# A mixture-of-factored-experts upper layer on TensorE: straight code that reads its operands in place, instead of loops that read staging buffers

## The chip, the cores and the metric

The kernel runs on one core of one Trainium2 chip. The metric is the device time of one launch in microseconds (us). The reference names used below are TensorE (PE, with PEld for its weight loads), VectorE (DVE), ScalarE (ACT), GpSimd (POOL) and SyncE (SP, which starts the DMA transfers). All data are float32.

## The reference

Three residual blocks follow each other: cross attention to a context, causal self attention, and a feed-forward part that is a mixture of experts with top-2 routing. Only the last is touched. Each of its two layers does this for every token:

```python
def kmoe(x_flat, W_router, A, B, scale, bias, d_in1, d_in2, d_out1, d_out2, top_k):
    logits = x_flat @ W_router.T
    vals, idx = jax.lax.top_k(logits, top_k)
    probs = jax.nn.softmax(vals, axis=-1)
    xs = x_flat.reshape(-1, d_in1, d_in2)
    Ag = A[idx]
    Bg = B[idx]
    Y = jnp.einsum('nkoi,nij,nkpj->nkop', Ag, xs, Bg)
    out = jnp.einsum('nkop,nk->nop', Y, probs).reshape(-1, d_out1 * d_out2)
    return out * scale + bias
...
h = kmoe(x_flat, W_up, A_up, B_up, scale_up, bias_up, D1, D2, F1, F2, TOP_K)
h = jax.nn.gelu(h, approximate=False)
y = kmoe(h, W_down, A_down, B_down, scale_down, bias_down, F1, F2, D1, D2, TOP_K)
```

There are 64 experts, D1 = D2 = 32 and F1 = F2 = 64. A pair of rows of 512 makes one item of 32x32, so there are 1024 items, of which the kernel takes 256 at a time: four blocks, T = 0 to 3.

## The kernel before

After the two attention stages (lines below 1230) comes `mixture`. Its **upper layer** runs over the four blocks T; its **lower layer** does so after it. For each block T of the upper layer TensorE does, in this order:

- **gather**: 16 units (`gather_up`, L2122), each of 32 small matmuls that multiply one-hot choices with the table of the factors A (v = 0) or B (v = 1), so that each item's factors appear in PSUM. ACT (L2006) and DVE (L1843) copy each unit out into the factor tiles `up[0]` and `up[1]`. A unit waits for the copies of the unit two before it.
- transposes of the next block's rows (`rows`, L1453), the router products of the lower layer for the block before (`logits_dn`, L2100) and of the upper layer for the next block (`logits_up`, L1460), and `fold_dn` (L2108);
- **steps**: 16 steps, two at a time. `first_up` (L2139) makes 64 small matmuls for two steps, ACT copies each result to `mid` (`mid_out`, L2022), `second_up` (L2157) makes 16 small matmuls for each step, DVE adds the bias (L1852), ACT applies gelu (L2033, L2027);
- transposes of the next choices (`transpose_choices`, L1468).

What is written once in the PE program and run in loops: the whole body for T (`pe.Fori(0, T_N)`), within it the gather (one lap is four units, four laps) and the steps (one lap is two steps, eight laps). Parts that some T does without stand in `pe.If`. Since a loop's body names fixed addresses, the operands that change from lap to lap come from **staging buffers** at fixed addresses: POOL copies four rows of the table into `tab_st` (`stage_table`, L1767), two rows of the factors into `st_a` and `st_b` for each step (`stage_a` L1775, `stage_b` L1784), and ACT copies the input's rows into `st_hh` (`stage_x`, L2014). PE waits for these copies on `s_ts`, `s_sta`, `s_stb` and `s_stx`. The cross attention before it is written out without loops on PE, self attention is one loop and one written-out last lap, and the lower layer is a loop again.

All orders are written by hand; each engine runs its own list, and semaphores tie them together.

Of the kernel before, what the change touches and what calls it, by code (L numbers as in the profile page):

```python
# [1243 lines left out]
def mixture_parts(sem, arena, over, area, low, top_area, early, ps, ident, h_at, tables):  # L1244
# [60 lines left out]
    s_xfe, s_gelu, s_stx = sem("mo_xfe"), sem("mo_gelu"), sem("mo_stx")  # L1305
# [11 lines left out]
    s_ts, s_ex, s_oc = sem("mo_ts"), sem("mo_ex"), sem("mo_oc")  # L1317
    s_sta, s_stb = sem("mo_sta"), sem("mo_stb")
# [229 lines left out]
    f.s_stx = s_stx  # L1548
# [18 lines left out]
    f.s_ts = s_ts  # L1567
    f.s_ex = s_ex
    f.s_oc = s_oc
    f.s_sta, f.s_sad, f.AHEAD = s_sta, s_sad, AHEAD  # L1570
# [29 lines left out]
def mixture(nc, block, arena, early, ps, a, first, rest, out):  # L1600
# [58 lines left out]
    s_stx = first.s_stx  # L1659
# [15 lines left out]
    s_ts = first.s_ts  # L1675
    s_ex = first.s_ex
    s_oc = first.s_oc
    s_sta, s_sad, AHEAD = first.s_sta, first.s_sad, first.AHEAD
# [27 lines left out]
    def _(sp):  # L1706
# [28 lines left out]
        sp.wait_ge(s_stx, STEPS * T_N + AHEAD)  # L1735
# [18 lines left out]
    def _(pool):  # L1754
# [8 lines left out]
        def stage_table(T, q):  # L1763
            for v in range(2):
                if T or q:
                    pool.wait_ge(s_gu, 16 * T + 2 * (q - 1) + v + 1)
                pool.tensor_copy(tab_st[v], tab_up[v][:, 4 * q:4 * q + 4, :]).then_inc(s_ts, 1)  # L1767

        def stage_a(T, n):
            if n == 0:  # L1770
                for e in range(2):
                    pool.wait_ge(s_geu[e], 16 * T + 15 + CREDIT)
            if T or n >= 2:
                pool.wait_ge(s_s1, STEPS * T + n - 1)
            pool.tensor_copy(four(st_a[n % 2]), up[0][:, :, rows_of(n), :].rearrange("p m r o -> p m (r o)"))\  # L1775
                .then_inc(s_sta, 1)

        def stage_b(T, n):
            if n == 0:
                for e in range(2):  # L1780
                    pool.wait_ge(s_geu[e], 16 * T + 16 + CREDIT)
            if T or n >= 2:
                pool.wait_ge(s_s2, STEPS * T + n - 1)
            pool.tensor_copy(four(st_b[n % 2]), up[1][:, :, rows_of(n), :].rearrange("p m r o -> p m (r o)"))\  # L1784
                .then_inc(s_stb, 1)

# [14 lines left out]
        pool.sem_inc(s_sta, AHEAD)  # L1801
        pool.sem_inc(s_stb, AHEAD)
        pool.memset(euler, EULER).then_inc(s_fold, 1)
        stage_table(0, 0)
        pool.wait_ge(s_fold, 2)
        exponential("up", 0)
        for T in range(T_N):
            for q in range(1, 8):
                stage_table(T, q)
            stage_a(T, 0)  # L1810
            stage_a(T, 1)
            for n in range(STEPS):
                stage_b(T, n)
                if n + 2 < STEPS:
                    stage_a(T, n + 2)
                if n == 6 and T + 1 < T_N:
                    exponential("up", T + 1)
                if n == 10 and T:
                    exponential("dn", T - 1)
                if n == 8 and T == 0:  # L1820
                    rest.rstd(pool)
            if T + 1 < T_N:
                stage_table(T + 1, 0)
# [9 lines left out]
    def _(vec):  # L1833
# [23 lines left out]
        def gather_out_dn(T, v, g):  # L1857
            if g == 1:
                if T and v == 0:
                    vec.wait_ge(s_sad, UP + STEPS * T + AHEAD - 2)  # L1860
                else:
                    vec.wait_ge((s_sta, s_stb)[v], UP + STEPS * T + AHEAD)
# [137 lines left out]
    def _(act):  # L2000
        def gather_out(T, q, v):
            if T and q == 0:
                act.wait_ge((s_sta, s_stb)[v], STEPS * T + AHEAD)
# [3 lines left out]

        def stage_x(T, n):

            if n == 0:  # L2010
                act.wait_ge(s_xt, 2 * T + 2)
            if T or n >= 2:
                act.wait_ge(s_s1, STEPS * T + n)
            act.copy(st_hh.rearrange("p (u z) -> p u z", u=2)[:, :, 0:P].rearrange("p u (t x) -> p u t x", t=2),  # L2014
                     xt[:, :, 2 * n:2 * n + 4, :].rearrange("p t (u r) j -> p u t (r j)", u=2)).then_inc(s_stx, 2)
# [19 lines left out]
        def gather_out_dn(T, v, g):  # L2035
            if g == 0:
                if T and v == 0:
                    act.wait_ge(s_sad, UP + STEPS * T + AHEAD - 2)
                else:
                    act.wait_ge((s_sta, s_stb)[v], UP + STEPS * T + AHEAD)  # L2040
# [12 lines left out]
        act.sem_inc(s_stx, AHEAD)  # L2053
        act.sem_inc(s_sad, UP + AHEAD - 2)
        act.sem_inc(s_ohe["dn"][0], CREDIT)
        for T in range(T_N):
# [3 lines left out]
            stage_x(T, 0)  # L2060
# [33 lines left out]
    def _(pe):  # L2094
# [16 lines left out]
        def gather_up(v, g):  # L2111

            pe.wait_ge(s_ts, g * 2 + v + 1)
            for e in range(2):
                pe.wait_ge(s_geu[e], g * 2 + v - 1 + CREDIT)
            apart(pe, SPARE)
            for o in range(4):
                for c in range(C):
                    for hf in range(2):
# [3 lines left out]
                                         tab_st[v][r, o, :], x, start=True, stop=True)  # L2123
            last.then_inc(s_gu, 1)

        def first_up(n):


            pe.wait_ge(s_sta, n + 2 + AHEAD)
            pe.wait_ge(s_stx, n + 2 + AHEAD)  # L2130
            apart(pe, SPARE)
            for u in range(2):
                xs = st_h[u][:, 0:P].rearrange("p (m j) -> p m j", m=4)
                for m in range(4):
                    for c in range(C):
# [203 lines left out]
```

## Time and profile before

| | us |
|---|---|
| median of 3 runs | 1332.3 (1331.91 to 1333.19) |
| the profiled execution, whole | 1332.9 |
| its span on the core | 1330.9 |
| PE busy within the span | 1239.7 |
| DVE, ACT, POOL busy | 809.8, 439.1, 227.8 |
| first to last instruction of the upper layer on PE | 868.7 to 1115.7 |

The rows are in the section after the change. Times of rows count from the span's start. On PE a matmul of float32 appears in the trace as two MATMUL records and two LDWEIGHTS records (the 2048 matmuls of L2122 are 4096 records of each kind), a transpose as one of each. "Idle before <-issue" means that the engine stood still and no semaphore, DMA or other engine that the profile shows had just released it. Queue q8 in the DMA part carries packets of kind "instruction".

### The profile page before, as it was taken

To read this page: it belongs to the slowest core of one execution; us is meant where nothing else is said; L and a number is where in the kernel's file an instruction comes from. 1 tells how busy PE (TensorE), PEld (TensorE's weight loads), DVE (VectorE), ACT (ScalarE), POOL (GpSimd) and SP (SyncE) were. 2 spreads that over 40 slices of the span, in tenths; PEclk is the share of its full clock that TensorE was granted. 3 is DMA by queue.
4 is the path that set the end of the run, shared out by engine and by line. 5 is a ranking of instruction groups with operands and counts; after the bars stand their busy time and mean duration, and the time that the engine had idled before them with its cause. 6 is when DMAs were issued, how large, how long until landed. Compare 5 with 4: busy or idle time off the path is not lost.

```text
span 1330.9 us, 61276 instructions
## 1 busy us (share of the span) xinstructions
PE 1239.7 (93%) x27820; PEld 808.8 (61%) x27820; DVE 809.8 (61%) x1523; ACT 439.1 (33%) x863; POOL 227.8 (17%) x373
## 2 busy tenths in 40 slices
PE   9999999999999999999999997978889888889886
PEld 6764333333333334677666774757778777779775
DVE  5567767767777771555565564546574846464766
ACT  2223211321132112222122221235463646354564
POOL 1000000000000001222122221116151532212212
PEclk9899999999999999999999999998999999895998
DMA  7976899899989973411101112201221306334012
GB/s 295 319 225 190 310 297 311 277 316 288 311 276 316 293 273 90 80 64 63 48 16 63 63 47 70 57 33 80 111 114 43 127 4 249 139 149 190 26 37 95
DMA packets 68176, 211.50 MB, mean 159 GB/s; under 512 B 14544, under 2 KB 30928, under 8 KB 53616
## 3 DMA queue, kind: packets, MB, share of 16 engines
q1 hardware_dynamic: 68080, 210.16, 46.9%
q8 instruction: 68, 1.11, 0.4%
q14 instruction: 28, 0.23, 0.1%
HBM read 172.37 MB, written 37.75 MB: 158 GB/s over the span
## 4 chain that ended last, share of the span: by engine, by line
PE 77%; DVE 10%; issue 5%; DMA 3%; POOL 2%; ACT 2%; SPq 1%; DVEq 0%; POOLq 0%; ACTq 0%
PE ps L715 14%; PE ps L564 10%; PE ps L1088 8%; PE ps L2171 6%; PE ps L235 4%; PE ps L2122 4%; PE ps L1202 4%; PE ps L1109 4%; DVE arena L576 4%; PE ps L479 3%; PE ps L2100 2%; PE ps L2213 2%; PE ps L705 2%; PE ps L2197 2%; DVE arena L1852 2%
## 5 line engine op out<-in xcount | busy, mean ns | idle before, releaser
L576 DVE STREAM_TRANSPOSE arena<-arena 128x448 f32<-128x448 f32 (+1 forms) x512 | 263.6, 577 | 101.8 <-PE ps L564 83.6
L564 PE MATMUL ps<-arena 32*64 32x400 f32 (+1 forms) x4096 | 202.7, 506 | 1.4 <-DVE arena L576 0.7
L715 PE MATMUL ps<-arena 128*64 128x512 f32 x832 | 189.2, 598 | 0.0
L564 PEld LDWEIGHTS ps<-arena 32*64 32x64 f32 x4096 | 75.3, 130 | 97.8 <-issue 51.7
L715 PEld LDWEIGHTS ps<-arena 128*64 128x64 f32 x832 | 55.6, 136 | 121.3 <-issue 111.9
L599 ACT ACTIVATE arena<-ps,arena 128x384 f32<-128x384 f32 x64 | 36.3, 582 | 276.5 <-DVE arena L590 276.5
L1088 PE MATMUL ps<-arena 128*128 128x256 f32 x512 | 114.7, 382 | 0.8 <-ACT arena L1023 0.8
L1088 PEld LDWEIGHTS ps<-arena 128*128 128x128 f32 x512 | 96.9, 191 | 17.4 <-issue 3.3
L2022 ACT COPY arena<-ps 128x512 f32<-128x512 f32 x128 | 75.1, 588 | 84.8 <-PE ps L2171 58.7
L1852 DVE SCALAR_TENSOR_TENSOR arena<-ps,arena 128x512 f32<-128x512 f32 x64 | 69.8, 1116 | 43.8 <-PE ps L2157 43.5
L2171 PE MATMUL ps<-arena 64*64 64x32 f32 x4096 | 84.2, 236 | 5.8 <-issue 5.7
L888 POOL TENSOR_TENSOR arena<-arena 128x1024 f32<-128x1024 f32 x8 | 18.9, 2367 | 406.5 <-PE ps L715 406.5
L2171 PEld LDWEIGHTS ps<-arena 64*64 64x64 f32 x4096 | 78.0, 153 | 10.2 <-issue 7.3
L2122 PE MATMUL ps<-arena 64*32 64x128 f32 x4096 | 69.1, 273 | 13.0 <-issue 6.7
L2122 PEld LDWEIGHTS ps<-arena 64*32 64x32 f32 x4096 | 58.1, 105 | 24.4 <-issue 19.6
L956 DVE SCALAR_TENSOR_TENSOR arena<-ps,arena 128x512 f32<-128x512 f32 x32 | 20.6, 686 | 81.0 <-PE ps L1099 81.0
L1791 POOL COPY arena<-arena 128x512 f32<-128x512 f32 x64 | 41.9, 659 | 162.1 <-ACT arena L2043 89.7
L2197 PE MATMUL ps<-arena 64*64 64x256 f32 x1024 | 62.1, 395 | 6.0 <-DVE arena L1865 3.5
L479 PE MATMUL ps<-arena 128*128 128x256 f32 x256 | 60.5, 391 | 0.0
L1843 DVE COPY arena<-ps 128x512 f32<-128x512 f32 x64 | 43.7, 692 | 27.1 <-PE ps L2122 26.9
L235 PE MATMUL ps<-arena 128*128 128x512 f32 x128 | 60.2, 605 | 0.0
L906 POOL TENSOR_TENSOR arena<-arena 128x512 f32<-128x512 f32 x32 | 33.4, 1044 | 149.3 <-DVE arena L973 149.3
(153 smaller groups left out, 1842.6 us busy)
## 6 DMA issues: line engine op xcount, KB each, us to landing
arena<-ctx SPq DMA_DIRECT2D x64, 1024.0 KB
arena<-ctx SPq DMA_DIRECT2D x32, 768.0 KB
arena<-q_n SPq DMA_DIRECT2D x64, 256.0 KB, 11.3
h_n<-arena SPq DMA_DIRECT2D x16, 1024.0 KB, 4.4
arena<-h_n SPq DMA_DIRECT2D x16, 1024.0 KB, 10.0
arena<-x SPq DMA_DIRECT2D x16, 512.0 KB, 4.5
arena<-ctx SPq DMA_DIRECT2D x32, 256.0 KB
x_n<-arena SPq DMA_DIRECT2D x16, 512.0 KB, 3.5
```

The costliest lines, as they stand in the source:

```text
L235: x = pe.matmul(ps[:, par, :], early.ats[:, c, par::2], early.xwv[:, c, :], start=c == 0, stop=c == DC - 1)
L479: last = pe.matmul(ps[:, QB + h, m % 2 * QROWS:(m % 2 + 1) * QROWS], wqk[:, c, m * P:(m + 1) * P], lnt[n][:, c, :], start=c == 0, stop=c = ...
L564: last = pe.matmul(ps[b * SEQ:(b + 1) * SEQ, tb, 0:WIDTH[tb]], qs[p % 2][r, db, b * SEQ:(b + 1) * SEQ], z[r, at % RING, b, 0:WIDTH[tb]], s ...
L576: vec.transpose(z[:, at % RING, :, g * 224:g * 224 + nt * 32].rearrange("p b (j t) -> p b j t", t=32), slots[slot_of(k)][:, :, 0:nt, db * ...
L715: last = pe.matmul(ps[b * SEQ:(b + 1) * SEQ, OB, :], probt[:, j, b * SEQ:(b + 1) * SEQ], slot[:, b, jj, :], start=j == 0, stop=j == TILES - 1)
L1088: last = pe.matmul(ps[:, bank, m % 2 * QROWS:(m % 2 + 1) * QROWS], w[n][:, c, m * P:(m + 1) * P], lnt[:, c, :], start=c == 0, stop=c == DC ...
L1109: last = pe.matmul(ps[e * SEQ:(e + 1) * SEQ, 2 + pair, s2 * 256:(s2 + 1) * 256], lnt[:, c, at:at + SEQ], w["swv"][:, c, :].rearrange("p (m ...
L1852: vec.scalar_tensor_tensor(h[:, q, :, at].rearrange("p j g -> p g j"), ps[:, b:b + 2, :].rearrange("p b (g x) -> p (b g) x", x=2 * F1)[:, ...
L2022: act.copy(mid[u].rearrange("p (b x) -> p b x", b=2), ps[:, 2 * u:2 * u + 2, 0:256]).then_inc(s_me, 1)
L2122: last = pe.matmul(ps[c * R:(c + 1) * R, 4 * v + hf, o * P:(o + 1) * P], tab_st[v][r, o, :], x, start=True, stop=True)
L2171: last = pe.matmul(ps[k * F1:(k + 1) * F1, 2 * u + t, g * D1:(g + 1) * D1], st_h[u][rows_t, g * F1:(g + 1) * F1], two(st_a[u])[rows_t, k, ...
L2197: last = pe.matmul(ps[t * E:(t + 1) * E, 2 * (g % 4) + hf, o % 2 * 2 * P:(o % 2 + 1) * 2 * P], tab_dn[v][r, o, :], x, start=True, stop=True)
```

## The change

On PE the loops over T, over the gather's units and over the steps, and the `If`s, are replaced by Python loops, so that every matmul of the upper layer stands in the program by itself, with its own addresses. `gather_up` then reads the tables `tab_up` directly, `first_up` reads `xt` and `up[0]`, and `second_up` reads `up[1]`. The copies `stage_table`, `stage_a`, `stage_b` (POOL) and `stage_x` (ACT) go, and with them the semaphores `s_ts`, `s_sta`, `s_stx`; those who waited on them to know that a buffer is free wait for `s_s1` and `s_s2`, the ends of the first and second products. The number and shape of the matmuls stays. The lower layer keeps its loops and its staging.

```diff
         def transposed(vec, T, t):
-            vec.wait_ge(s_stx, STEPS * T + AHEAD)
+            vec.wait_ge(s_s1, STEPS * T)
...
-            for q in range(1, 8):
-                stage_table(T, q)
-            stage_a(T, 0)
-            stage_a(T, 1)
-            for n in range(STEPS):
-                stage_b(T, n)
-                if n + 2 < STEPS:
-                    stage_a(T, n + 2)
...
-                vec.wait_ge((s_sta, s_stb)[v], STEPS * T + AHEAD)
+                vec.wait_ge((s_s1, s_s2)[v], STEPS * T)
...
-            stage_x(T, 0)
-                if n + 2 < STEPS:
-                    stage_x(T, n + 2)
...
-        def gather_up(v, g):
-            pe.wait_ge(s_ts, g * 2 + v + 1)
+        def gather_up(T, v, q):
             for e in range(2):
-                pe.wait_ge(s_geu[e], g * 2 + v - 1 + CREDIT)
-            apart(pe, SPARE)
+                pe.wait_ge(s_geu[e], 16 * T + 2 * q + v - 1 + CREDIT)
...
-                                         tab_st[v][r, o, :], x, start=True, stop=True)
+                                         tab_up[v][r, 4 * q + o, :], x, start=True, stop=True)
...
-        def first_up(n):
-            pe.wait_ge(s_sta, n + 2 + AHEAD)
-            pe.wait_ge(s_stx, n + 2 + AHEAD)
+        def first_up(T, n):
+            u = n % 2
+            if n == 0:
+                pe.wait_ge(s_xt, 2 * T + 2)
...
-        def second_up(n, u):
-            pe.wait_ge(s_stb, n + 1 + AHEAD)
...
-                                             four(st_b[u])[rows_d, 2 * t + c, r * F1:(r + 1) * F1], start=True, stop=True)
+                                             up[1][rows_d, 2 * t + c, 2 * n + r, :], start=True, stop=True)
...
         def steps_up(T):
-            with pe.Fori(T * 8, T * 8 + 8) as i:
-                first_up(i * 2)
-                second_up(i * 2, 0)
-                second_up(i * 2 + 1, 1)
+            for n in range(0, STEPS, 2):
+                first_up(T, n)
+                first_up(T, n + 1)
+                second_up(T, n)
+                second_up(T, n + 1)
...
-        with pe.Fori(0, T_N) as T:
+        for T in range(T_N):
...
-            with pe.Fori(T * 4, T * 4 + 4) as j:
-                for r in range(2):
-                    gather_up(0, j * 2 + r)
-                    gather_up(1, j * 2 + r)
+            for q in range(8):
+                for v in range(2):
+                    gather_up(T, v, q)
...
-            with pe.If(T < T_N - 1):
+            if T + 1 < T_N:
```

What stands in PE's program for the gather and the steps before, written once for all four blocks (`ps` is PSUM, `arena` is SBUF; L2122 is the gather, L2139 and L2157 the two products):

```order
L2248 ISA
L2115 REGISTER_ALU
L2122 MATMUL ps<-arena 32x128 x32
L2113 REGISTER_ALU
...
L2248 COMPARE_AND_BRANCH
...
L2219 ISA
L2139 MATMUL ps<-arena 32x64 x64
L2146 REGISTER_ALU
L2157 MATMUL ps<-arena 64x64 x32
L2219 ISA
L2219 COMPARE_AND_BRANCH
```

The same place in the changed kernel, for block T = 1 (L2071 is the gather, L2051 `logits_dn`, L2086 and L2101 the two products):

```order
L2071 MATMUL ps<-arena 32x128 x512
L1453 MATMUL ps<-arena 128x128 x16
L2051 MATMUL ps<-arena 64x128 x128
L1460 MATMUL ps<-arena 128x64 x16
L2059 MATMUL ps<-arena 128x64 x2
L2086 MATMUL ps<-arena 32x64 x64
L2101 MATMUL ps<-arena 64x64 x32
L2086 MATMUL ps<-arena 32x64 x64
L2101 MATMUL ps<-arena 64x64 x32
```

Branches and register instructions are gone from this part; the gather stands there as 512 matmuls in a row where 4 times 32 stood, and the pair of products eight times where it stood once, and all of it once more for each T.

POOL's program in one block T before (L1767 copies the table, L1775 and L1784 the factors, L1761 is the exponential of a routing):

```order
L1767 COPY arena<-arena 128x128 x16
L1775 COPY arena<-arena 128x512 x2
L1784 COPY arena<-arena 128x512
L1775 COPY arena<-arena 128x512
L1784 COPY arena<-arena 128x512
```

and all that POOL has left to do in the changed kernel's upper layer:

```order
L1774 MEMSET arena 128x2
L1757 TENSOR_TENSOR arena<-arena 128x2 x2
L150 TENSOR_SCALAR arena<-arena 128x2
L152 TENSOR_TENSOR arena<-arena 128x2
L1757 TENSOR_TENSOR arena<-arena 128x2 x5
```

The exponentials and the last attention lap's small statistics stay; every copy between them is gone.

## Rows read from the trace of the kernel before

**Rows 1.** The page: busy time (share of the span) xinstructions by engine

```profile
PE 1239.7 (93%) x27820; PEld 808.8 (61%) x27820; DVE 809.8 (61%) x1523; ACT 439.1 (33%) x863; POOL 227.8 (17%) x373
```

**Rows 2.** Busy time in stretches: attention, then the upper layer's T = 0 to 3

```profile
core 0: us, PE busy (x) PEld busy (x) DVE busy (x) ACT busy (x) POOL busy (x), PEclk, DMA share, GB/s
24.00:560.00 536.00, 528.51 (x5962) 244.66 (x5961) 344.94 (x740) 126.96 (x353) 16.27 (x24) 0.99 0.83 265
868.60:935.30 66.70, 50.59 (x2617) 44.83 (x2616) 36.52 (x57) 33.93 (x56) 26.35 (x51) 0.92 0.16 64
935.30:996.30 61.00, 55.16 (x2884) 49.11 (x2884) 37.99 (x63) 33.17 (x57) 24.24 (x50) 1.00 0.26 104
996.30:1058.00 61.70, 55.09 (x2884) 49.11 (x2884) 38.90 (x65) 33.77 (x58) 24.25 (x50) 1.00 0.22 85
1058.00:1114.00 56.00, 47.89 (x2822) 42.43 (x2822) 34.53 (x49) 30.34 (x51) 23.12 (x47) 1.00 0.19 75
1196.00:1230.00 34.00, 33.71 (x1365) 31.90 (x1369) 17.10 (x29) 14.74 (x27) 10.12 (x16) 0.52 0.46 179
```

**Rows 3.** PE in order of time, T = 1: start, us, line, records [idle before]

```profile
935.36 4.49 PE L2122 MATMUL ps<-arena 64*32 64x128 f32 x256 [1.53 <-DVE arena L1438]
...
950.37 4.25 PE L2122 MATMUL ps<-arena 64*32 64x128 f32 x256 [0.28 <-issue]
...
968.17 1.48 PE L2139 MATMUL ps<-arena 32*32 32x64 f32 x128
969.80 1.32 PE L2157 MATMUL ps<-arena 64*64 64x64 f32 x64
...
992.78 0.69 PE L2157 MATMUL ps<-arena 64*64 64x64 f32 x32 [0.26 <-DVE arena L1852]
```

**Rows 4.** PE in order of time, T = 0, the loop's first lap

```profile
868.65 2.76 PE L2122 MATMUL ps<-arena 64*32 64x128 f32 x153
874.14 1.89 PE L2122 MATMUL ps<-arena 64*32 64x128 f32 x103 [2.72 <-issue]
...
897.39 6.88 PE L1460 MATMUL ps<-arena 128*128 128x64 f32 x32 [5.38 <-issue]
```

**Rows 5.** The same view at the upper layer's end and in the lower layer

```profile
1115.69 14.86 PE L2197 MATMUL ps<-arena 64*64 64x256 f32 x240 [0.77 <-ACT arena L1440]
...
1144.26 0.43 PE L2213 MATMUL ps<-arena 128*32 128x32 f32 x12 [1.74 <-issue]
```

**Rows 6.** DMA queues in the stretch 24 to 560: packets, MB, share

```profile
q8 instruction: 47, 0.77, 0.6%
```

**Rows 7.** DMA queues in the stretch 936 to 1113 (all that there are)

```profile
q1 hardware_dynamic: 2569, 15.60, 22.1%
q14 instruction: 6, 0.05, 0.1%
```

**Rows 8.** DMA from 891.6 to 895.0, to 895.3, to 898.5, to 898.8

```profile
q8 instruction: 1, 0.02, 2.1%
...
q8 instruction: 2, 0.03, 3.8%
...
q8 instruction: 2, 0.03, 2.0%
...
q8 instruction: 3, 0.05, 3.0%
```

**Rows 9.** PE in order of time, logits of T = 1 at full clock

```profile
956.81 7.27 PE L2100 MATMUL ps<-arena 64*64 64x128 f32 x256
964.01 3.79 PE L1460 MATMUL ps<-arena 128*128 128x64 f32 x32
```

**Rows 10.** Groups by line: busy us, mean ns | idle before it, releasers

```profile
L2122 PE MATMUL ps<-arena 64*32 64x128 f32 x4096 | 69.1, 273 | 13.0 <-issue 6.7 <-DVE arena L1843 4.3 <-DVE arena L1438 1.5
```

**Rows 11.** One copy that goes, and further down who waited for it

```profile
L1784 POOL COPY arena<-arena x64: 604/618/625, 890.7 to 1109.3; 128x512 f32<-128x512 f32 x64
...
  PE ps L2157: 5.2, 7
```

More of the change, by code:

```diff
@@ L1674, in mixture @@
     s_ohe = first.s_ohe
-    s_ts = first.s_ts
     s_ex = first.s_ex
     s_oc = first.s_oc
-    s_sta, s_sad, AHEAD = first.s_sta, first.s_sad, first.AHEAD
+    s_sad, AHEAD = first.s_sad, first.AHEAD
     s_stb = first.s_stb
@@ L1734, in _ @@
                 sp.wait_ge(s_out, QUADS * 32)
-        sp.wait_ge(s_stx, STEPS * T_N + AHEAD)
+        sp.wait_ge(s_s1, STEPS * T_N)
         for q in range(4):
@@ L1761, in exponential @@
             pool.tensor_tensor(ex[k], euler, diff[k], ALU.pow).then_inc(s_ex, 1)
[L1763 to L1785, printed above, removed]
         def stage_b_dn(T, n):
@@ L1807, in _ @@
         for T in range(T_N):
-            for q in range(1, 8):
-                stage_table(T, q)
-            stage_a(T, 0)
-            stage_a(T, 1)
-            for n in range(STEPS):
-                stage_b(T, n)
-                if n + 2 < STEPS:
-                    stage_a(T, n + 2)
[L1816 to L1821, printed above, removed]
-            if T + 1 < T_N:
-                stage_table(T + 1, 0)
+            if T + 1 < T_N:
+                exponential("up", T + 1)
+            if T == 0:
+                rest.rstd(pool)
+            if T:
+                exponential("dn", T - 1)
         for T in range(T_N):
@@ L1858, in gather_out_dn @@
             if g == 1:
-                if T and v == 0:
+                if T == 0:
+                    vec.wait_ge((s_s1, s_s2)[v], UP)
+                elif v == 0:
                     vec.wait_ge(s_sad, UP + STEPS * T + AHEAD - 2)
                 else:
-                    vec.wait_ge((s_sta, s_stb)[v], UP + STEPS * T + AHEAD)
+                    vec.wait_ge(s_stb, UP + STEPS * T + AHEAD)
             vec.wait_ge(s_gd[v], 8 * T + g + 1)
@@ L2002, in gather_out @@
             if T and q == 0:
-                act.wait_ge((s_sta, s_stb)[v], STEPS * T + AHEAD)
+                act.wait_ge((s_s1, s_s2)[v], STEPS * T)
             act.wait_ge(s_gu, 16 * T + 2 * q + v + 1)
@@ L2036, in gather_out_dn @@
             if g == 0:
-                if T and v == 0:
+                if T == 0:
+                    act.wait_ge((s_s1, s_s2)[v], UP)
+                elif v == 0:
                     act.wait_ge(s_sad, UP + STEPS * T + AHEAD - 2)
                 else:
-                    act.wait_ge((s_sta, s_stb)[v], UP + STEPS * T + AHEAD)
+                    act.wait_ge(s_stb, UP + STEPS * T + AHEAD)
             act.wait_ge(s_gd[v], 8 * T + g + 1)
@@ L2122, in gather_up, with second_up @@
                         last = pe.matmul(ps[c * R:(c + 1) * R, 4 * v + hf, o * P:(o + 1) * P],
-                                         tab_st[v][r, o, :], x, start=True, stop=True)
+                                         tab_up[v][r, 4 * q + o, :], x, start=True, stop=True)
             last.then_inc(s_gu, 1)
-        def first_up(n):
-            pe.wait_ge(s_sta, n + 2 + AHEAD)
-            pe.wait_ge(s_stx, n + 2 + AHEAD)
[L2131 to L2135, printed above, removed]
-                        rows_c = slice(c * R, (c + 1) * R)
-                        for k in range(2):
-                            q = 2 * (c % 2) + k
-                            last = pe.matmul(ps[q * R:(q + 1) * R, 2 * u + c // 2, m * F1:(m + 1) * F1],
-                                             xs[rows_c, m, :],
-                                             four(st_a[u])[rows_c, m // 2 * 2 + k, m % 2 * F1:(m % 2 + 1) * F1],
-                                             start=True, stop=True)
-                last.then_inc(s_s1, 1)
-        def second_up(n, u):
-            pe.wait_ge(s_me, n + 1 + AHEAD)
-            pe.wait_ge(s_stb, n + 1 + AHEAD)
-            pe.wait_ge(s_bias, n + 1 + AHEAD)
-            apart(pe, SPARE)
+        def first_up(T, n):
+            u = n % 2
+            if n == 0:
+                pe.wait_ge(s_xt, 2 * T + 2)
+            for m in range(4):
+                t, row = m // 2, 2 * n + m % 2
+                for c in range(C):
+                    rows_c = slice(c * R, (c + 1) * R)
+                    for k in range(2):
+                        q = 2 * (c % 2) + k
+                        last = pe.matmul(ps[q * R:(q + 1) * R, 2 * u + c // 2, m * F1:(m + 1) * F1],
+                                         xt[rows_c, t, row, :], up[0][rows_c, 2 * t + k, row, :], start=True, stop=True)
+            last.then_inc(s_s1, 1)
+        def second_up(T, n):
+            u = n % 2
+            pe.wait_ge(s_me, STEPS * T + n + 1 + AHEAD)
+            pe.wait_ge(s_bias, STEPS * T + n + 1 + AHEAD)
             for c in range(2):
```

36 lines of the change are left out of this document (10 added, 26 removed).

## The prediction, made before the changed kernel was run

> **What bounds the kernel now.** I read the busy times first, then the upper layer lap by lap, then PE's own order of instructions, then the DMA queues. PE is busy for 93% of the span [rows 1], and in the four blocks of the upper layer for 50.6, 55.2, 55.1 and 47.9 us of 66.7, 61.0, 61.7 and 56.0 us [rows 2]. DVE and ACT are busy for under two thirds there, POOL for under half. So PE sets the pace of the upper layer, and POOL's copies matter only where PE waits for them. The whole layer takes 1115.7 - 868.7 = 247 us [rows 4, 5].
>
> What sort of work PE does there decides this case. In the gather 256 MATMUL records take 4.25 us [rows 3], each with its weight load: 512 instructions, 8.3 ns each. The first products take 1.48 us for 128 records, the second 1.32 us for 64 [rows 3]: 384 instructions in 2.8 us, 7.3 ns each. These are the smallest matmuls of the kernel. In the cross attention, which is written out, PE ran 5962 + 5961 instructions in 536 us, 45 ns each [rows 2].
>
> **Where the instructions come from.** In those 536 us queue q8 brought 47 packets with 0.77 MB [rows 6]. That is 16.4 KB for 11923 / 47 = 254 instructions, so about 64 bytes each and one packet for each block of 256. Between 936 and 1113, while PE ran through its loops, the queue brought nothing at all [rows 7]: a loop's body, once fetched, stays. Only the first laps fetch, and there PE stands still without a releaser: in the first gather after 153 records, for 2.72 us; before the first L1460, for 5.38 us; in the lower layer before L2213, for 1.74 us [rows 4, 5]. In the second of these the DMA engines had almost nothing else to do, and the packets came one by one, the second after 895.0 and the third after 898.5, some 3.5 us apart [rows 8]. So the next block is not asked for early enough to run ahead of code this dense. In the cross attention a block lasted 536 / 47 = 11.4 us, which hid any fetch; code of 8.3 ns an instruction is through a block in 2.1 us.
>
> **The change, part by part.**
>
> 1. *The code is written out.* In the changed program each T has 512 gather matmuls and 8 times 64 + 32 = 768 of the steps. Four instructions each: 4 x 1280 x 4 = 20480, or 80 blocks of 256 that run once and must each be fetched. (Logits, transposes and waits are some 8 blocks more.) Today these parts take, for T = 1, 19.2 us (935.4 to 954.6) and 25.3 us (968.2 to 993.5) [rows 3]; with the longer T = 0 about 184 us for all four. The rest of the layer, 247 - 184 = 63 us, is logits, transposes and waits.
>
> What one fetched block costs is bounded from both sides. Low: the 5.38 us of idle before L1460 hold two fetches, 2.7 us each [rows 4]. High: the first gather ran 306 instructions in 2.76 + 2.72 = 5.48 us, or 4.6 us for 256 [rows 4]. Between them stands the distance of packets, 3.5 us [rows 8]. I take 3.7 us: that distance is the nearest to a steady chain of fetches, and a little more because h's stores, 4 MB in each T, keep the DMA engines busy for a fifth of the time (0.16 to 0.26 [rows 2]). So 80 x 3.7 = 296 us instead of 184: **+112 us**. By the ends, 216 and 368 us. As the fetch takes longer than the instructions (2.1 us in the gather, 1.9 us in the steps), PE's own work is hidden behind it, not added.
>
> 2. *The rest of the layer.* T = 0 loses the 5.38 us of idle before L1460 and the slow clock behind it (6.88 us for 32 records where T = 1 needs 3.79 [rows 4, 9]): -8.5 us. Logits of the lower layer last 7.27 us for two blocks [rows 9], 3.6 us a block, so a fetch just keeps up with them. Transposes and logits give the next block time to arrive, worth up to 2 or 3 us in all. 63 - 8.5 - 2.5 = 52 us: **-11 us**.
>
> 3. *The staging copies go.* POOL loses nearly all of its 26.4 + 24.2 + 24.3 + 23.1 = 98 us there [rows 2], ACT one short copy for every two steps. What PE waited for them is 5.2 us before L2157 [rows 11], inside the 184 us, and the fetch covers it. Nothing is left of this gain while part 1 holds.
>
> 4. *Loop overhead and waits.* Of the 13.0 us idle before L2122, 6.7 are "issue" (2.72 the stall of T = 0, the others about 0.3 us at the loop's edges) and 4.3 the wait for DVE's copies [rows 10]. These too lie inside the 184 us and vanish behind the fetches. The new waits on `s_s1` and `s_s2` ask for results of the block before, which the engines have long consumed: nothing. The exponentials, which stood behind up to two copies on POOL, come a little sooner; nobody on the path waits for them.
>
> 5. *After the upper layer.* The lower layer's program is the same; it starts later by the sum. Its load of h waits for the last gelu as before.
>
> Sum against the profiled execution: 1332.9 + 112 - 11 = 1433.9, and as its median of runs is 0.6 us lower, **1433 us**. With 2.7 us a block the sum gives 1354, with 4.6 us 1506.
>
> **The Trainium skill on this point.** "Runtime: NRT & Kernel Launch", section "Instruction fetch mechanics", says that the sequencer fetches the next page while it executes the current one, that crossing a page is mostly hidden because issue is slower than the fill, and that a taken branch out of the window is what stalls, so that kernels prefer full unrolling. By that rule this change is right and the first rival below holds. The page's unit of 256 instructions agrees with the trace [rows 2, 6]; its statement that issue is slower than the fill does not, where PE issues an instruction in 8 ns.
>
> **Rivals.**
>
> *The fetch runs ahead in straight code (faster).* The stalls of rows 4 stand near branches; the cross attention, straight for 47 packets, shows none. If the sequencer asks for blocks early enough when nothing branches, PE is bound by its own work and gains what it waits for now: 2.7 + 5.4 us of fetches in T = 0, 3.1 us of slow clock, 5.6 us for POOL, some 4 us of loop edges: -21 us, 1312 us. It decides from a block cost below about 2.3 us (184 / 80). Against it: the first gather stalled 306 instructions after its entry, in the middle of a unit where no branch stands, though the program is sequential there; and in the cross attention one packet comes per block and 11.4 us cover any latency, so its silence proves nothing. The skill's rule named above is this rival.
>
> *The fetch is partly ahead.* Two requests overlap now and then, or PE's queue of issued instructions bridges a part: a block at 2.3 to 3.1 us, 80 x 2.7 = 216 us, 1354 us.
>
> *The clock falls as well.* With 2 us of work in 3.7 us PE would be busy for some 55% of the time. The granted clock was 0.52 from 1196 to 1230 [rows 2], behind waits that are shorter than this. At the lower of its two levels (1.2 and 2.4 GHz) the gather's 2.1 us a block would about double, to the length of the fetch, and hide there; logits would not: 3 x (7.3 + 3.8) us become up to twice that, +33 us, and some blocks outlast their fetch, another 20 us: 1486 us.
>
> *The change does not do what it says.* The order of instructions shows PE's code without a branch from T = 0 to T = 3 and all copies gone, so this is left at 1 in 100; the time would be within 0.2%.
>
> **How the numbers follow.** Block cost between 3.1 and 4.3 us, with or without a part of the clock's effect (1385 to 1485): 0.80. Partly ahead, 1340 to 1385: 0.06. Clock falls throughout, or the high end of the block cost, above 1485: 0.05. Fetch hidden, 1300 to 1325: 0.08. No effect: 0.01. The predicted time is the first case's, 1433 us; the range 1383 to 1485 leaves out the other cases, together 0.2. Faster by over 0.2% (about what a measurement of this kernel can tell from no change): 0.08; within: 0.01; slower: 0.91.
>
> **What would show it.** In the profile after: q8 with some 82 packets more than before, nearly one for each block from 869 on; the four blocks of the upper layer at 75 to 90 us each; PE's idle before the gather put down to issue, one gap of 1 to 2 us for each 128 records; POOL almost without work until the lower layer; the gather's PE busy time unchanged. Wrong if gather units follow each other at 2.1 us for 128 records with packets 2.1 us apart: then the fetch keeps pace, and the first rival has it. Part 2 is wrong if the granted clock of the stretch is far below 1.

## The result

The changed kernel takes 1457.6 us (median, 1456.9 to 1458.6), the kernel before 1332.1 us beside it: a ratio of 1.0945, with a 95% interval of 1.0929 to 1.096. It is slower by 125 us. The prediction was 1433 us with a range of 1383 to 1485 us. The profiled executions of two experiments below, t_out (1376.9 us) and lap4 (1375.7 us), were 14 and 9 us longer than any other execution of the same kernels, at a lower granted clock.

The page of the changed kernel, span and busy times, and the instruction queue (against [rows 1]):

```profile
span 1454.9 us, 60553 instructions
...
PE 1284.1 (88%) x27820; PEld 837.3 (58%) x27820; DVE 806.4 (55%) x1523; ACT 428.6 (29%) x831; POOL 135.7 (9%) x181
...
q8 instruction: 150, 2.46, 0.7%
```

PE ran the same 27820 + 27820 records as before, in 124 us more. POOL lost 92 us of work and ACT 32 instructions, to no use. Queue q8 carried 150 packets where it carried 68 in all before.

Busy times by stretch, the four blocks T of the upper layer, with the same columns as [rows 2]:

```profile
868.40:956.40 88.00, 61.31 (x2623) 52.24 (x2626) 36.40 (x57) 31.13 (x48) 1.62 (x3) 0.75 0.13 51
956.40:1052.60 96.20, 67.76 (x2884) 59.38 (x2884) 36.13 (x63) 30.48 (x49) 1.38 (x2) 0.77 0.19 69
1052.60:1150.50 97.90, 68.32 (x2890) 59.66 (x2891) 38.09 (x65) 31.39 (x50) 1.38 (x2) 0.81 0.15 57
1150.50:1244.60 94.10, 61.84 (x2829) 52.65 (x2829) 34.43 (x49) 28.91 (x44) 0.69 (x1) 0.77 0.14 54
```

The stretches grew from 66.7, 61.0, 61.7 and 57.7 us (the last one up to 1115.7) to 88.0, 96.2, 97.9 and 94.1 us. PE's busy share fell from 76 to 90% to about 70%, and the granted clock from 0.92 to 1.00 down to 0.75 to 0.81.

PE in order of time, in the gather of T = 0 (against [rows 4], and [rows 3] for the loop in steady state):

```profile
877.72 2.38 PE L2071 MATMUL ps<-arena 64*32 64x128 f32 x127 [0.23 <-issue]
881.68 2.37 PE L2071 MATMUL ps<-arena 64*32 64x128 f32 x127 [1.58 <-issue]
885.44 2.38 PE L2071 MATMUL ps<-arena 64*32 64x128 f32 x127 [1.39 <-issue]
889.49 2.38 PE L2071 MATMUL ps<-arena 64*32 64x128 f32 x127 [1.67 <-issue]
893.19 2.39 PE L2071 MATMUL ps<-arena 64*32 64x128 f32 x127 [1.32 <-issue]
```

127 MATMUL records, their 127 weight loads and two waits are the 256 instructions of one block. PE is through them in 2.4 us and then stands still for 1.3 to 1.7 us with no releaser; a block comes every 3.7 to 4.1 us. PE starts again 2.2 to 3.0 us after the packet of its block has started (median 2.4, of the 56 stalls over 0.9 us in the upper layer). Where [rows 3] shows 256 records in a piece, here the pieces end at the block's edge, wherever in a unit that falls. The gaps by line, as time idle before each group:

```profile
L2071 PE MATMUL ps<-arena 64*32 64x128 f32 x4096 | 81.8, 298 | 44.5 <-issue 41.7 <-DVE arena L1803 0.8 <-ACT arena L1968 0.7
L2086 PE MATMUL ps<-arena 32*32 32x64 f32 x4096 | 67.7, 275 | 42.9 <-issue 42.9
L2101 PE MATMUL ps<-arena 64*64 64x64 f32 x2048 | 62.6, 290 | 24.4 <-issue 23.7
```

Of 111.8 us idle before these three lines, 108.3 are "issue". DVE's wait before L2122 in [rows 10], 4.3 us, is down to 0.8, and no line of the upper layer waits for POOL. The 88 packets of the upper layer, in the DMA view of the stretch 868.4 to 1244.6:

```profile
q8 instruction: 88, 1.44, 1.6%
```

### The profile page after: what moved, and what is told of

It reads as the page before. It is cut to its first block, busy times and chain, and to the rows that moved or that the text cites. A ratio compares the mean times of both kernels' runs of the same rounds, so it can differ in the third digit from the quotient of the medians.

```text
span 1454.9 us, 60553 instructions
## 1 busy us (share of the span) xinstructions
PE 1284.1 (88%) x27820; PEld 837.3 (58%) x27820; DVE 806.4 (55%) x1523; ACT 428.6 (29%) x831; POOL 135.7 (9%) x181
## 4 chain that ended last, share of the span: by engine, by line
PE 79%; issue 10%; DVE 6%; DMA 2%; ACT 1%; POOL 0%; SPq 0%; DVEq 0%; POOLq 0%; ACTq 0%
PE ps L715 12%; PE ps L564 9%; PE ps L1088 7%; PE ps L2071 5%; PE ps L2115 5%; PE ps L2101 4%; PE ps L2086 4%; PE ps L235 4%; DVE arena L576 4%; PE ps L1202 4%; PE ps L1109 4%; PE ps L479 3%; PE ps L2141 3%; PE ps L2051 2%; PE ps L2157 2%
## 5 line engine op out<-in xcount | busy, mean ns | idle before, releaser
L1975 ACT COPY arena<-ps 128x512 f32<-128x512 f32 x128 | 75.1, 587 | 177.4 <-PE ps L2086 121.4
L2071 PE MATMUL ps<-arena 64*32 64x128 f32 x4096 | 81.8, 298 | 44.5 <-issue 41.7
L1088 PE MATMUL ps<-arena 128*128 128x256 f32 x512 | 115.7, 384 | 0.8 <-ACT arena L1023 0.8
L2086 PE MATMUL ps<-arena 32*32 32x64 f32 x4096 | 67.7, 275 | 42.9 <-issue 42.9
L2071 PEld LDWEIGHTS ps<-arena 64*32 64x32 f32 x4096 | 67.1, 115 | 59.6 <-issue 51.1
L2115 PE MATMUL ps<-arena 64*64 64x32 f32 x4096 | 80.7, 231 | 5.4 <-issue 5.0
L2086 PEld LDWEIGHTS ps<-arena 32*32 32x32 f32 x4096 | 54.9, 129 | 52.3 <-issue 49.0
L2101 PE MATMUL ps<-arena 64*64 64x64 f32 x2048 | 62.6, 290 | 24.4 <-issue 23.7
L2115 PEld LDWEIGHTS ps<-arena 64*64 64x64 f32 x4096 | 74.5, 147 | 9.5 <-issue 6.7
L2101 PEld LDWEIGHTS ps<-arena 64*64 64x64 f32 x2048 | 54.0, 195 | 32.4 <-issue 28.4
L1968 ACT COPY arena<-ps 128x512 f32<-128x512 f32 x64 | 38.7, 605 | 90.2 <-PE ps L2071 90.2
```

What stands on the lines that cost most here:

```text
L1088: last = pe.matmul(ps[:, bank, m % 2 * QROWS:(m % 2 + 1) * QROWS], w[n][:, c, m * P:(m + 1) * P], lnt[:, c, :], start=c == 0, stop=c == DC ...
L1975: act.copy(mid[u].rearrange("p (b x) -> p b x", b=2), ps[:, 2 * u:2 * u + 2, 0:256]).then_inc(s_me, 1)
L2071: last = pe.matmul(ps[c * R:(c + 1) * R, 4 * v + hf, o * P:(o + 1) * P], tab_up[v][r, 4 * q + o, :], x, start=True, stop=True)
L2086: last = pe.matmul(ps[q * R:(q + 1) * R, 2 * u + c // 2, m * F1:(m + 1) * F1], xt[rows_c, t, row, :], up[0][rows_c, 2 * t + k, row, :], st ...
L2101: last = pe.matmul(ps[t * F1:(t + 1) * F1, 4 + 2 * u + d, to:to + F1], mid[u][rows_d, at:at + F1], up[1][rows_d, 2 * t + c, 2 * n + r, :], ...
L2115: last = pe.matmul(ps[k * F1:(k + 1) * F1, 2 * u + t, g * D1:(g + 1) * D1], st_h[u][rows_t, g * F1:(g + 1) * F1], two(st_a[u])[rows_t, k, ...
```

## Experiments

The table gives, from the traces, the time between the first and the last record of each gather and of each block's 16 steps on PE, the whole upper layer (up to the first record of the lower layer), and its packets in q8. In the changed kernel a block of T has 8 blocks of instructions in its gather and 12 in its steps.

| kernel | gathers, T = 0 to 3 | steps, T = 0 to 3 | upper layer | q8 packets in it |
|---|---|---|---|---|
| before | 21.1, 19.3, 19.8, 19.8 | 28.6, 25.3, 25.3, 24.6 | 247.0 | 6 |
| changed | 32.0, 30.1, 32.7, 30.8 | 46.4, 50.6, 48.5, 48.7 | 376.3 | 88 |
| straight_staged | 32.3, 33.0, 31.3, 32.3 | 49.5, 48.3, 44.7, 50.1 | 378.6 | 89 |
| gather_straight | 31.8, 31.9, 33.6, 28.9 | 28.7, 25.4, 26.8, 26.7 | 287.3 | 47 |
| t_out | 21.9, 20.8, 26.1, 23.4 | 28.7, 25.4, 25.4, 24.7 | 250.3 | 22 |
| lap4 | 22.1, 25.8, 23.3, 23.0 | 31.4, 29.9, 29.0, 30.0 | 286.4 | 38 |
| quiet | 29.2, 28.6, 30.3, 29.0 | 41.5, 43.2, 44.1, 43.9 | 345.5 | 88 |
| pool_order | 22.0, 19.2, 19.9, 19.8 | 27.4, 24.6, 24.6, 24.2 | 244.5 | 6 |
| peel_pool | 22.2, 24.0, 19.8, 22.5 | 26.5, 24.7, 24.7, 24.8 | 247.6 | 19 |
| peel_pad | 22.4, 24.9, 19.8, 19.8 | 27.2, 26.0, 24.7, 24.1 | 250.8 | 11 |

### straight_staged: only the code written out

```diff
-        with pe.Fori(0, T_N) as T:
+        for T in range(T_N):
...
-            with pe.Fori(T * 4, T * 4 + 4) as j:
+            for j in range(T * 4, T * 4 + 4):
...
-            with pe.If(T > 0):
+            if T > 0:
...
-            with pe.Fori(T * 8, T * 8 + 8) as i:
+            for i in range(T * 8, T * 8 + 8):
```

> The kernel before, with PE's upper layer written out like in the changed kernel (no loop, no branch), but every staging copy, its semaphore and the reads from the staging buffers kept. Theory fetch (PE stands still for its own next block of instructions): the time of the changed kernel, 1458 us give or take 8, with some 82 packets more in queue q8 than before and gaps of 1 to 2 us every 128 MATMUL records. Rival in place (reading the table, x and the factors where they lie, or the new waits on s_s1 and s_s2, makes PE slow): the time before, 1332 us give or take 8.

Measured: 1463.5 us (1452.2 to 1469.4), ratio 1.0993 (1.0929 to 1.1057). The copies are all there, POOL is busy for 230.2 us of the span, and the time is that of the changed kernel; the single stretches of the table agree within 4 us. The groups of its trace:

```profile
L2122 PE MATMUL ps<-arena 64*32 64x128 f32 x4096 | 83.4, 296 | 46.5 <-issue 43.6 <-ACT arena L1440 1.0 <-POOL arena L1767 0.4
```

So the whole loss comes from writing PE's code out. Reading in place, and the waits that came with it, make no difference beyond the 6 us between the two medians.

### gather_straight: only the gathers written out

As straight_staged, but the steps keep their `pe.Fori`.

> The kernel before, with the loop over T and the loop of the gather written out; the steps keep their loop of two steps a lap, and all staging stays. Only the gather's 4 x 8 blocks of 256 instructions become code that runs once. Theory fetch: the gathers grow from some 20 to some 31 us each and the steps stay at 25 to 28 us, so 1332 + 4 x 11 + a few for the first laps of the steps, less 8 for the jump of T = 0 that is gone: 1370 to 1385 us. If the cost lay in the loops' absence as such, or in the steps alone, 1335 us.

Measured: 1371.7 us (1369.7 to 1378.1), ratio 1.0324 (1.029 to 1.0359). The gathers went to 29 to 34 us, 46 us more in all; the steps, still loops, stayed where they were. The dose goes with the number of blocks that run once: 32 of the 80 blocks, 40 of the 125 us (the stall of T = 0 before L1460, which this kernel also loses, makes it a little less).

### t_out: only the outer loop written out

```diff
-        with pe.Fori(0, T_N) as T:
+        for T in range(T_N):
...
-            with pe.If(T < T_N - 1):
+            if T < T_N - 1:
...
-            with pe.If(T > 0):
+            if T > 0:
```

> The kernel before, with only the loop over T and its branches written out; within each T the gather and the steps stay loops. Some 16 blocks more are fetched than before. Theory fetch: each T now has first laps, where the gather's loop (two blocks) and the steps' loop (one and a half) run into their fetches, some 5 us for each of T = 1 to 3, and T = 0 loses the stall of 5.4 us and the slow clock of 3.1 us at its jump: 1333 to 1342 us. If writing out a loop costs for another reason than fetches (for instance branches that let queues settle), the cost should be a good part of the 125 us, over 1360 us.

Measured: 1358.3 us (1352.2 to 1376.9), ratio 1.0194 (1.0153 to 1.0236). This missed both expectations, and the table says where: the upper layer took 250.3 us, 3.3 more than before, as the theory has it. In the profiled execution the loss is in the lower layer, which nobody had touched: 255.8 us in place of 215.2. Its packets in q8, from the upper layer's end to the end of the span, before and here:

```profile
q8 instruction: 11, 0.18, 0.4%
```

```profile
q8 instruction: 26, 0.43, 0.7%
```

PE's program became 4060 instructions longer, all of them in the upper layer (21568 in place of 17508 for the whole), and the lower layer's loop, 1630 instructions or 6.4 blocks, moved from blocks 62.1 to 68.5 to blocks 77.97 to 84.3. (Places are the instruction's number in PE's program over 256, shifted by 27 instructions, as the first stalls show.) It used to touch 7 blocks, now 8, and with the next one, if PE asks for it at the loop's end, nine. That this is why it fetched more fits the packets but was argued from these places, which are good to a few instructions only (77.97 lies eight before a block's edge).

Nor are the fetches the greater part of the loss in this trace. The lower layer:

```profile
1119.10:1374.90 255.80, 213.67 (x7436) 188.04 (x7436) 129.24 (x188) 107.62 (x165) 44.68 (x71) 0.71 0.27 103
```

Beside 182.1 us of PE busy at a granted clock of 0.87 in the kernel before, the same 7436 records kept PE busy for 213.7 us at 0.71. That is 31.5 of the 40.6 us; the time in which PE was not busy grew by 9.1 us, and the fetches can account for no more than that directly. The other executions of this kernel (1352.2 to 1362.5 us) ran at 0.951 to 0.961 of the clock over their whole length, where the kernel before had 0.966 to 0.975, so part of their loss is the clock's too. Whether the stalls brought the clock down was not tested.

### lap4: a loop that is a little too long

```diff
-            with pe.Fori(T * 8, T * 8 + 8) as i:
-                first_up(i * 2)
-                second_up(i * 2, 0)
-                second_up(i * 2 + 1, 1)
+            with pe.Fori(T * 4, T * 4 + 4) as i:
+                for k in range(2):
+                    first_up(i * 4 + 2 * k)
+                    second_up(i * 4 + 2 * k, 0)
+                    second_up(i * 4 + 2 * k + 1, 1)
```

> The kernel before with four steps in a lap of the steps' loop instead of two; staging and all else the same. The body of T grows from 1611 to 1995 instructions, from 6.3 to 7.8 blocks of 256, and with its place in the program it now lies over 9 blocks where it lay over 8. If PE holds no more than 8 blocks, at least a part of the body is fetched again in each T, with packets between 936 and 1113 where there were none before, and 5 us more for each of T = 1 to 3: about 1347 us. If it holds more: no packets there, and half the loop edges gone, 1330 to 1333 us.

Measured: 1363.9 us (1354.6 to 1375.7), ratio 1.0229 (1.0184 to 1.0273). Slower by 33 us where some 15 were expected, with no work added. Where the loops before fetched nothing between 936 and 1113 [rows 7], this kernel fetched in the stretch 925 to 1154:

```profile
q8 instruction: 31, 0.51, 0.9%
```

Its body touches 9 blocks, and each of the laps T = 1 to 3 fetched ten: the nine again, and one more. PE at the start of T = 1:

```profile
940.15 1.09 PE L2122 MATMUL ps<-arena 64*32 64x128 f32 x28 [3.87 <-issue]
945.02 3.75 PE L2122 MATMUL ps<-arena 64*32 64x128 f32 x125 [3.78 <-issue]
949.34 1.89 PE L2122 MATMUL ps<-arena 64*32 64x128 f32 x103 [0.57 <-issue]
```

Two stalls of 3.8 us stand there, and every first pass over the steps' body pays again. But the upper layer as a whole, before and here, shows two costs:

```profile
868.70:1115.70 247.00, 209.56 (x11214) 186.15 (x11214) 148.63 (x231) 132.28 (x221) 97.96 (x198) 0.98 0.21 82
```

```profile
867.70:1154.10 286.40, 226.75 (x11213) 200.66 (x11213) 148.64 (x231) 132.01 (x221) 98.17 (x198) 0.88 0.18 72
```

Of 39.4 us more, 22.2 are time in which PE was not busy, and 17.2 are the same work at a granted clock of 0.88. The other executions (1354.6 to 1366.4 us, at 0.962 to 0.968 over their whole length) lost less to the clock, and how their 33 us divide was not profiled.

### quiet: the fetch without other traffic

```diff
-                sp.dma_start(a["h"][T, q, :, :], h[:, q].rearrange("p j n -> p (j n)")).then_inc(s_hd, 16)
+                sp.dma_start(a["h"][T, q, :, 0:16], h[:, q].rearrange("p j n -> p (j n)")[:, 0:16]).then_inc(s_hd, 16)
```

The loads of h and of the next rows are cut in the same way, so that later blocks compute on stale data and only the upper layer's time is compared.

> The changed kernel with the DMA traffic of the feed-forward part cut to 64 bytes a row: the stores and loads of h and the loads of the next rows move 16 of their 2048 columns. Later blocks then compute on stale data, and the lower layer no longer waits for its loads of h; only the upper layer's time is to be compared. In the changed kernel a block of instructions takes 4.0 us in gathers and steps, by packet distances 3.8 us where the DMA engines are quiet and 4.8 us where they carry a store. Theory: the fetch shares its way with the other transfers, and the upper layer falls from 376 us to about 360 us (80 blocks at 3.8 us and 56 us of the rest). If the traffic does not matter it stays at 376 us give or take 4. In both cases it stays far above the 247 us of the kernel before.

Measured: the upper layer took 345.5 us in place of 376.3. Gathers and steps are 117.1 + 172.7 = 289.8 us, 3.62 us for each of the 80 blocks, where the changed kernel needs 4.0. (Between packets, within a gather or the steps, the mean distance is 3.8 us; a stage with 8 or 12 packets in it has 7 or 11 such distances and a shorter rest at its two ends, so its time per block is a little less.) Its stretch has the DMA share 0.03:

```profile
868.20:1213.70 345.50, 250.75 (x11213) 214.93 (x11213) 145.18 (x231) 121.67 (x189) 5.06 (x8) 0.82 0.03 8
```

The fetch and the kernel's own transfers do get in each other's way, for 30 us of the 125, twice what was expected. In the changed kernel, single distances between packets show it too, 72 of them within gathers and steps: with the DMA engines under 10% busy they are 3.7 us in the mean (55 of them), as in quiet, and with over 30% busy 5.3 us (16; the expectation had 4.8).

### wide_loop and wide_straight: the same code with longer work

```diff
-                        last = pe.matmul(ps[c * R:(c + 1) * R, 4 * v + hf, o * P:(o + 1) * P],
+                        last = pe.matmul(ps[c * R:(c + 1) * R, 4 * v + hf, :],
```

with a moving operand of 512 columns, in the kernel before (wide_loop) and in gather_straight (wide_straight). Both compute something else than the reference; only their gathers are compared.

> The kernel before with each matmul of the upper layer's gather 512 columns wide instead of 128: the same number of instructions, each of longer work; its results are not the reference's. Pair of the next run. A unit of 32 such matmuls should take 3.4 to 4.4 us instead of 1.1, so each gather of 16 units 55 to 70 us; only the gathers are to be compared with the next run.

> The same wide matmuls in the run gather_straight, where the gather stands written out (64 matmuls, two units, to a block of 256 instructions). With 128 columns the written-out gathers took 31.5 us against 20 us in the loop. Theory fetch: a block now works for 7 us or more, longer than the 4 us of a fetch, so the gathers take the same time as in wide_loop, give or take 2 us, with no gaps. If straight code is slow for another reason that goes with each instruction or each unit, they stay 11 us longer each.

Measured: all eight gathers, four in each kernel, took 55.2 us. Their groups, wide_loop first:

```profile
L2122 PE MATMUL ps<-arena 64*32 64x512 f32 x4096 | 220.7, 589 | 2.1 <-DVE arena L1438 1.6 <-issue 0.5
```

```profile
L2122 PE MATMUL ps<-arena 64*32 64x512 f32 x4096 | 220.7, 589 | 1.0 <-DVE arena L1438 1.0
```

Same number of instructions, same code written out, same packets (47 in the upper layer, as in gather_straight), and no gap: a block of two units now works for 55.2 / 8 = 6.9 us. Even the stall in the loop's first lap (2.72 us in [rows 4]) is gone. This settles that it is the rate of instructions against the rate of the fetch, and nothing in straight code as such.

### pool_order: what the staging really cost

```diff
-                if n == 6 and T + 1 < T_N:
+                if n == 7 and T + 1 < T_N:
                     exponential("up", T + 1)
-                if n == 10 and T:
+                if n == 11 and T:
                     exponential("dn", T - 1)
-                if n == 8 and T == 0:
+                if n == 9 and T == 0:
                     rest.rstd(pool)
```

> The kernel before with three small pieces of POOL's work moved by one step (the exponentials from behind step 6 to behind step 7 and from 10 to 11, the last attention statistics from 8 to 9), to where POOL waits for PE anyway; loops and staging are kept. PE waited 5.2 us before the second products for the copies behind these pieces. If that is what the staging costs, those waits go and the time falls by 2 to 5 us, to some 1328 us, which is all that reading in place could have won on POOL's side. If something else is late next (DVE's bias), within 1 us of before.

Measured: 1325.8 us (1323.4 to 1329.6) beside 1331.45 for the kernel before, ratio 0.9964 (0.9952 to 0.9977). What L2157 waited for (us, times; POOL stood at 5.2, 7 in [rows 11]):

```profile
  DVE arena L1852: 1.9, 6
  ACT arena L2022: 0.9, 1
  POOL arena L1784: 0.7, 2
```

The steps became 3.0 us shorter over the four blocks (table) and the upper layer 2.5 us; the median says 5.7 for the whole kernel, and what made the rest was not looked into. The waits for POOL were not the price of staging itself, only of three pieces of other work in the way of it. Moving three lines took 4.5 of the 5.2 us of waits for POOL away, with the loops kept; 1.0 us of it came back as waits for DVE's bias.

### peel_pool and peel_pad: T = 0 by itself, and where the loop lies

```diff
-        with pe.Fori(0, T_N) as T:
+        for T in range(1):
...
+        with pe.Fori(1, T_N) as T:
```

with the body written twice and its `If`s resolved; peel_pad adds, behind the transposes of T = 0,

```diff
+                for _ in range(pad):
+                    pe.wait_ge(early.s_t, 14 * 16)
```

> The order of the run before it, and T = 0 of the upper layer written out ahead of a loop over T = 1 to 3, each with its inner loops. The jump over the lower layer's router products in T = 0 goes, with its 5.4 us of idle and some 3 us of slow clock; the first laps of T = 1 now wait for their instructions once more, 4 to 5 us. The loop over T lies over blocks 55.8 to 62.06, eight blocks with 15 instructions in the last. If PE does not ask for block 63 from there, the time falls by another 4 us, to about 1324 us. If it does, blocks are thrown out and fetched again in each lap, with packets in T = 2 and 3, and the time is above 1340 us.

> The run peel_pool with 116 waits that are long fulfilled (58 instructions) put where PE waits for ACT in T = 0 anyway. They move the loop over T = 1 to 3 from blocks 55.8 to 62.06 (eight blocks) to blocks 56.04 to 62.29 (seven). In peel_pool the loop's eight blocks and the one asked for behind them threw each other out once, before T = 3: 9 packets and some 3 us. Theory: packets of the upper layer fall from 19 to about 10, the gather of T = 3 from 22.5 to 20 us, the whole to about 1320 us, or up to 2 us more for the waits themselves. If place does not matter, 1323 us and the same packets.

Measured: peel_pool 1323.3 us (1318.7 to 1328.3), ratio 0.9938 (0.992 to 0.9955); peel_pad 1326.5 us (1318.9 to 1335.0) with ratio 0.9968 (0.9942 to 0.9995). Both beat the kernel before. Both also contain pool_order's three moved lines, and their intervals overlap with pool_order's 0.9952 to 0.9977. A gain from peeling T = 0 by itself (2.5 us between the medians of pool_order and peel_pool) is not shown; in the traces, the upper layer is 3 and 6 us longer than in pool_order. In peel_pool L1460 of T = 0 waits 1.14 us for ACT instead of the 5.38 us in [rows 4], and runs at full clock:

```profile
891.43 3.76 PE L1460 MATMUL ps<-arena 128*128 128x64 f32 x32 [1.14 <-ACT arena L1447]
```

But the loop was thrown out once, before T = 3, neither never nor in every lap, as had been expected:

```profile
1053.65 1.06 PE L2122 MATMUL ps<-arena 64*32 64x128 f32 x20 [3.69 <-issue]
1055.85 5.58 PE L2122 MATMUL ps<-arena 64*32 64x128 f32 x236 [1.13 <-issue]
```

With the loop's place moved, the packets fell from 19 to 11 and the gather of T = 3 from 22.5 to 19.8 us, as foreseen. Putting the waits there cost more than that:

```profile
897.88 7.03 PE L1460 MATMUL ps<-arena 128*128 128x64 f32 x32 [4.85 <-issue]
```

4.85 us of idle in place of 1.14, and the slow clock behind it. I had taken the waits to be covered by the wait for ACT; the stall was not. It need not be the waits themselves: the 58 instructions also moved the ends of the blocks, and in this gap, and not in peel_pool's, a packet of q8 started (at 894.8 us, 3.1 us before PE went on). Which of the two it was, was not tested.

## Why the prediction was right, and which terms were off

**The mechanism.** That PE would stand still for its next block of instructions was right. straight_staged puts the whole loss on the written-out code, gather_straight shows it growing with the blocks, and the wide pair makes it vanish when each block works longer than its fetch. Against the form foretold, the gaps (1 to 2 us every 128 records), the 82 more packets and POOL's empty stretch are as the last part of the prediction has them. Three signs are not. The blocks T were to take 75 to 90 us each and took 88 to 98. The gather's busy time was to be unchanged and rose from 69.1 to 81.8 us. And the granted clock fell to 0.75 to 0.81, which was named as the sign that part 2 is wrong; part 2 gained 7 us of its 11.

**The size.** The sum, set against the trace, in us:

| term | predicted | measured |
|---|---|---|
| gathers and steps, 184 before | 80 x 3.7 = 296, +112 | 319.8 = 80 x 4.0, +136 |
| rest of the layer, 63 before | 52, -11 | 56.5, -7 |
| lower layer, 215.2 before | 0 | 210.3, -5 |
| together | +101 | +124 |

The term that was mis-sized is the cost of a block. The distance of 3.5 us that I read from [rows 8] was nearly good: without other traffic a block costs 3.62 us (quiet). What I added for the stores of h, 0.2 us, is 0.4. The bound from below, 2.7 us, was a misreading: of the two packets in the idle time before L1460 the first had started before PE stood still (PE stopped at 892.0, the packet started at 891.7), so that time never held two whole fetches.

The rest of the layer was 4.5 us longer than foreseen. Of the 5.38 us of idle that were to go in T = 0, 1.0 stayed as a wait for ACT, which the fetch had hidden. The other 3.7 us are the transposes of the choices, most of which ran at the lower clock. Before and after the change:

```profile
L1468 PE MATMUL ps<-arena 128*128 128x128 f32 x64 | 8.8, 279 | 2.6 <-DVE arena L1852 2.6
```

```profile
L1468 PE MATMUL ps<-arena 128*128 128x128 f32 x64 | 12.5, 364 | 1.3 <-DVE arena L1812 1.3
```

**The lower layer** gained 5 us though its program is the same. Its granted clock rose from 0.87 to 0.90, rows of before and after the change:

```profile
1115.70:1330.90 215.20, 182.13 (x7436) 162.19 (x7436) 128.94 (x188) 107.94 (x165) 47.09 (x71) 0.87 0.31 122
```

```profile
1244.60:1454.90 210.30, 177.27 (x7436) 153.65 (x7436) 128.97 (x188) 107.84 (x165) 48.32 (x71) 0.90 0.31 123
```

Which moments are slow differs from kernel to kernel; why it was fewer here was not tested. No part of the prediction stands for these 5 us, so that they brought the sum nearer to the measurement is luck.

**The rivals.** That the fetch runs ahead in straight code is refuted; the rule of the Trainium skill behind it ("Runtime: NRT & Kernel Launch", section "Instruction fetch mechanics") does not hold on PE for code as dense as this, 7 to 8 ns an instruction against 3.62 us for 256 of them, 14 ns. That it is partly ahead is refuted by the same distance. The clock did fall, to 0.75 to 0.81, which I had given less weight as a case; but as the prediction argued for the gather, it hardly mattered there: of the 55 distances between packets with quiet DMA engines, 19 lay wholly at full clock with 3.77 us in the mean, 18 wholly at the lower one with 3.78 us. The 33 us that this rival put on the logits did not come: the router products of the lower layer (L2051) within the upper layer's time took 22.5 us of PE busy, where the kernel before needed 22.1, and L1460 took 11.3 in place of 14.5; both ran almost wholly at full clock. Rows of the changed kernel at full clock show the same period, 3.75 to 4.0 us from start to start:

```profile
1168.19 2.30 PE L2071 MATMUL ps<-arena 64*32 64x128 f32 x127 [1.63 <-issue]
1171.94 2.27 PE L2071 MATMUL ps<-arena 64*32 64x128 f32 x127 [1.45 <-issue]
1175.95 2.28 PE L2071 MATMUL ps<-arena 64*32 64x128 f32 x127 [1.74 <-issue]
```

**The gain that was hoped for.** Part 3 said that the staging's 5.2 us would vanish behind the fetch; straight_staged (1463.5 us, with staging) beside the change (1457.6 us, without) leaves 6 us between the medians, and their ranges overlap.

## What to carry to other kernels

Before a PE loop of small matmuls is written out, divide: here a block of 256 instructions took 3.6 to 4.0 us to arrive, so by estimate straight code is free only if each instruction works for 14 to 16 ns or more (a float32 matmul is four, so 56 to 64 ns; the experiments lie at 8 ns, where it is not free, and at 27 ns, where it is); below that keep the loop and feed it through fixed buffers. Keep a loop's body, its edges and, to be safe, the block behind it within eight blocks, and look at the instruction queue again after any edit upstream, since added code moves every later loop. And look first at who is late in the staging: moving three lines of another engine's program took away most of the waits that removing the copies aimed at, and kept the loops.

## What the runs showed of the hardware that I had not expected

- PE keeps about eight blocks of 256 instructions. The loop of the kernel before, which by my count of places ends within some ten instructions of the start of its eighth block, fetched nothing on later laps (0 packets in [rows 7]); a loop over nine fetched ten in every lap (31 packets in lap4), and the kernel took 33 us more of 1331, part of it through the clock.
- In between, the edge matters: peel_pool's loop, with 15 instructions in its eighth block by that count, was fetched again before one lap of the two that could have shown it; t_out's lower layer, which lies well into an eighth block, fetched 26 packets instead of 11. That PE also asks for the block behind the loop, and that this ninth one pushes out another, is the explanation that fits, not one that was shown.
- A place in the program can matter far away: t_out's lower layer is unchanged, and only the 4060 instructions ahead of it moved it. What these fetches cost is small beside what the lower clock cost in the same trace (9 us at most against 31).
- Instruction packets share their way with the kernel's transfers: 3.62 us a block with the DMA engines at a share of 0.03, 4.0 us at 0.13 to 0.19; single distances between packets are 3.7 us with the engines under 10% busy and 5.3 us with them over 30% busy.
- A stall ends 2.2 to 3.0 us after the start of the packet that it waits for, of which the packet itself takes 1.05 us (median); most packets start before PE has stopped, so a packet inside the gap is not a sign to rely on.
